# A transformer block on one core: channels in the order quad, dimension, head, a scratch layout to match, and another order of work ahead of the first quad

## The reference, cut to what matters

```python
x: (2, 1024, 128); 16 heads of 8
xn = layernorm(x)
Q, K, V = split_heads(xn @ wq.T), split_heads(xn @ wk.T), split_heads(xn @ wv.T)
Q, K = rope(Q), rope(K)                      # pairs (2f, 2f+1) of a head's 8 channels
attn = softmax(where(causal, Q K^T / sqrt(8), -inf))
out = x + (attn V) merged @ wo.T + (xn @ CB.T) * (SCB / 127) + bias
```

## Time and profile before

| | us |
|---|---|
| median of 3 runs | 284.9 (284.44 to 287.26) |
| profiled execution, its time | 284.91 |
| its span in the profile | 283.2 |
| mean granted TensorE clock | 0.994 of 2.4 GHz |

### The profile page before, as it was taken

How to read it: one execution, slowest core, us unless ns; L and a number is a source line. 1 busy time by engine, 2 the same in 40 slices (tenths; PEclk the granted TensorE clock), 3 DMA queues, 4 the chain that set the end, 5 groups by cost and what they waited for, 6 DMA issues and landing times.

```text
span 283.2 us, 11098 instructions
## 1 busy us (share of the span) xinstructions
PE 252.2 (89%) x4752; PEld 133.6 (47%) x4752; DVE 211.7 (75%) x601; ACT 188.6 (67%) x366; POOL 110.5 (39%) x170
## 2 busy tenths in 40 slices
PE   0785869759999999999999999999999999999875
PEld 0342644124334545554454554455455446666574
DVE  5897367878999899899798998988997783111123
ACT  0336423419877698779798789778988886888201
POOL 7634990499006561437440232043024014301200
PEclk9999999989999999999999999999999999999999
DMA  7415757480003450340043052005300000000011
GB/s 209 171 37 147 197 117 135 100 222 5 1 2 101 123 106 3 84 92 5 2 114 61 3 124 55 3 2 121 55 5 3 2 3 7 21 22 23 21 38 40
DMA packets 21497, 18.29 MB, mean 65 GB/s; under 512 B 2996, under 2 KB 20788, under 8 KB 21448
## 3 DMA queue, kind: packets, MB, share of 16 engines
q1 hardware_dynamic: 20872, 17.00, 25.1%
q10 hardware_dynamic: 576, 0.59, 0.7%
HBM read 12.12 MB, written 5.24 MB: 61 GB/s over the span
## 4 chain that ended last, share of the span: by engine, by line
PE 69%; DVE 13%; POOL 6%; DMA 5%; SPq 3%; ACT 2%; issue 2%; ACTq 0%; DVEq 0%
PE psV L908 21%; PE psB L840 19%; PE psA L840 18%; PE psA L943 7%; DVE prod L738 7%; DMA k_scratch<-ot 2%; DVE xn L696 2%; POOL xnT L440 2%; POOL ot L433 2%; SPq L336 2%; PE psB L823 1%; DMA x_sb<-x 1%; SPq L350 1%; DMA ks<-k_scratch 1%; DVE on L759 1%
## 5 line engine op out<-in xcount | busy, mean ns | idle before, releaser
L738 DVE CUSTOM_DVE_ANT_0 prod<-psA,cmask 128x128 f32<-128x128 f32 (+7 forms) x256 | 178.9, 755 | 28.8 <-PE psA L840 27.6
L641 ACT ACTIVATE ring<-psB 128x512 f32<-128x512 f32 x288 | 155.5, 601 | 33.2 <-PE psB L840 30.8
L840 PE MATMUL psB<-qs,ks 128*32 128x512 bf16 (+3 forms) x1536 | 101.7, 329 | 0.5 <-ACT maxT L600 0.4
L840 PE MATMUL psA<-ks,qs 128*32 128x512 bf16 (+3 forms) x1536 | 92.3, 330 | 7.9 <-DVE mx L738 4.3
L908 PE MATMUL psV<-ring,va 128*32 128x512 f32 (+3 forms) x768 | 76.1, 486 | 0.0
L487 POOL TENSOR_SCALAR_AFFINE_SELECT ring<-ring 128x512 f32<-128x512 f32 x64 | 39.9, 636 | 76.6 <-ACT ring L641 76.4
L840 PEld LDWEIGHTS psB<-qs,ks 128*32 128x32 bf16 x1536 | 41.3, 97 | 47.1 <-ACT ring L641 20.7
L840 PEld LDWEIGHTS psA<-ks,qs 128*32 128x32 bf16 x1536 | 34.0, 97 | 44.6 <-DVE mx L738 23.8
L908 PEld LDWEIGHTS psV<-ring,va 128*32 128x32 f32 x768 | 22.2, 110 | 16.0 <-issue 8.0
L467 POOL CAST shiftsT<-maxT 16x128 bf16<-16x128 f32 x16 | 4.5, 281 | 56.4 <-ACT maxT L633 50.1
L738 DVE DVE_READ_ACCUMULATOR2_ANT mx<- 128x1 f32 x256 | 21.4, 83 | 0.0
(11 more groups left out here) (88 smaller groups left out, 169.1 us busy)
## 6 DMA issues: line engine op xcount, KB each, us to landing
qs<-q_scratch SPq DMA_DIRECT2D x48, 96.0 KB
ks<-k_scratch SPq DMA_DIRECT2D x48, 96.0 KB
q_scratch<-ot SPq DMA_DIRECT2D x20, 128.0 KB, 2.7
k_scratch<-ot SPq DMA_DIRECT2D x12, 128.0 KB, 2.7
x_sb<-x SPq DMA_DIRECT2D x4, 256.0 KB, 4.6
rope_sb<-rope SPq DMA_DIRECT2D x2, 512.0 KB, 6.1
y<-xn SPq DMA_DIRECT2D x8, 128.0 KB, 1.8
qs<-shiftsT SPq DMA_DIRECT2D x32, 4.0 KB, 1.7
```

The source lines that it names most:

```text
L641: act.activation(ring[:, s % P_RING, k * HALF:(k + 1) * HALF], bank_b(e % B_RING), ACT.Exp)\
L738: last = dve.tensor_tensor_reduce(masked_scores[:, u % 2, at:at + w], psA[:, (u % 2) * SEQ + at:(u % 2) * SEQ + at + w], cmask[:, SEQ - w: ...
L840: mm = pe.matmul(psum[strip:strip + STRIP, at:at + size], keys[:, strip:strip + STRIP], queries, start=True, stop=True)
```

## The change

- *Channels.* Within the 128 channels of Q and K the order becomes quad, dimension, head (`rows` in the host's weights, the rope table with it). The scratch tensors become [token block, quad, part, 32 channels, 512 tokens], so that for one dimension the 4 heads are consecutive and a stack's row is one piece of 4 KB in DRAM.
- *Stores.* Each part is written once: 6 transfers a round, [4 quads, 32, 512].
- *Loads.* A half stack is 4 transfers: one per query part with its 8 rows repeated to 24 by a broadcast source, and one for the keys, 24 rows repeated to 72.
- *Order.* The weights 4 to 6, `scb` and `bias` are issued by SP behind rope, not by ACT. PE projects round 0 before it turns group 1, and does the first task (now V of batch 0) before groups 2 and 3. DVE normalises groups 2 and 3 between the rotations. POOL makes `cmask` first, scales the FFN's weights between the third and fourth rstd, and has pads of slots 1 and 2 and `va` behind the third parts. The tasks' table and `TASK_AFTER` are rewritten.

```diff
-TASKS = [("late", 4), ("late", 5), ("v", 0), ("v", 1), ("ffn", 0), ("ffn", 1), ("late", 6), ("max", 0), ("late", 7),
+TASKS = [("v", 0), ("ffn", 0), ("late", 4), ("late", 5), ("v", 1), ("ffn", 1), ("late", 6), ("max", 0), ("late", 7),
...
-        scratch = (nc.dram_tensor("q_scratch", [HEADS, PARTS + 2, DH, BATCH * SEQ], BF16),
-                   nc.dram_tensor("k_scratch", [HEADS, PARTS, DH, BATCH * SEQ], BF16))
+        scratch = [nc.dram_tensor(f"{name}_scratch", [BATCH * SEQ // HALF, HEADS // QUAD, PARTS, DH * QUAD, HALF], BF16)
+                   for name in ("q", "k")]
...
-            return 16 * (2 * PARTS * (i // SLOTS + 1) + i // SLOTS)
+            return 16 * (STACK_DMAS * (i // SLOTS + 1) + i // SLOTS)
...
-        ROUND_DMAS = 2 * PARTS + 2
+        ROUND_DMAS = 2 * PARTS
+        STACK_DMAS = PARTS + 1
...
-                for m in (n, PARTS + n) if c % 2 == 0 and n < 2 else (n,):
-                    sp.dma_start(scratch[c % 2][:, m, :, tok:tok + HALF], part(c, n)).then_inc(scratch_out[c // 2], 16)
+                sp.dma_start(scratch[c % 2][c // 2, :, n, :, :], part(c, n)).then_inc(scratch_out[c // 2], 16)
...
+                queries = scratch[0][block, rows, :, :, :].rearrange("p (d h) t -> p d (h t)", h=QUAD)
                 for g in range(PARTS):
-                    for source, first, stack in ((scratch[0], g, qs), (scratch[1], 0, ks)):
...
+                    sp.dma_start(qs[g * GROUP:(g + 1) * GROUP, slot, hf, :, :].rearrange("r h t -> r (h t)"),
+                                 queries[g, :, :].unsqueeze(0).to_broadcast([PARTS, DH, QUAD * HALF])).then_inc(ready, 16)
+                keys = scratch[1][block, rows, :, :, :].rearrange("p (d h) t -> (p d) (h t)", h=QUAD)
+                sp.dma_start(ks[0:STACK, slot, hf, :, :].rearrange("r h t -> r (h t)"),
+                             keys.unsqueeze(0).to_broadcast([PARTS, GROUP, QUAD * HALF])).then_inc(ready, 16)
...
             normalise(0)
+            normalise(1)
             statistics(2)
-            normalise(1)
-            statistics(3)
-            normalise(2)
-            normalise(3)
...
+            rotate(0)
+            rotate(1)
+            leave(0)
+            leave(1)
+            normalise(2)
+            statistics(3)
+            rotate(2)
+            normalise(3)
+            rotate(3)
+            leave(2)
+            leave(3)
...
             turn_rows(0)
-            turn_rows(1)
             pe.wait_ge(wq_scaled, 1)
             project_round(0)
+            turn_rows(1)
             project_round(1)
...
+        d = ch // QUAD % DH
...
+    rows = np.arange(P).reshape(HEADS // QUAD, QUAD, DH).transpose(0, 2, 1).reshape(P)
+    swap = rows ^ 1
```

More of the change, by code:

```diff
@@ L264, in attention_ffn_kernel @@
         cb_scaled = sem("cb_scaled")
+        va_set = sem("va_set")
         ln_step = sem("ln_step")
@@ L329, in _ @@
                 sp.dma_start(rope_sb[:, :, cols], rope[:, :, cols]).then_inc(rope_in[half], 16)
+            sp.dma_start(w_sb[:, 4:7, :], weights[:, 4:7, :]).then_inc(w_late_in, 16)
+            sp.dma_start(scb_sb[:, :], scb.partition_broadcast(P)).then_inc(vec_in, 16)
+            sp.dma_start(bias_sb[:, :], bias.partition_broadcast(P)).then_inc(vec_in, 16)
             def store_part(c, n):
-                tok = c // 2 * HALF
                 sp.wait_ge((part1, part2, part3)[n], c + 1)
-                for m in (n, PARTS + n) if c % 2 == 0 and n < 2 else (n,):
-                    sp.dma_start(scratch[c % 2][:, m, :, tok:tok + HALF], part(c, n)).then_inc(scratch_out[c // 2], 16)
+                sp.dma_start(scratch[c % 2][c // 2, :, n, :, :], part(c, n)).then_inc(scratch_out[c // 2], 16)
             def store_parts(r):
@@ L344, in load_stack @@
             def load_stack(i, hf):
-                slot, heads, tok = i % SLOTS, slice((i % 4) * QUAD, (i % 4 + 1) * QUAD), (i // 4) * SEQ + hf * HALF
+                slot, rows, block = i % SLOTS, i % 4, (i // 4) * 2 + hf
                 ready = stack_in[slot][hf]
+                queries = scratch[0][block, rows, :, :, :].rearrange("p (d h) t -> p d (h t)", h=QUAD)
                 for g in range(PARTS):
-                    for source, first, stack in ((scratch[0], g, qs), (scratch[1], 0, ks)):
-                        sp.dma_start(stack[g * GROUP:(g + 1) * GROUP, slot, hf, :, :],
-                                     source[heads, first:first + PARTS, :, tok:tok + HALF]
-                                     .rearrange("h p d t -> (p d) h t")).then_inc(ready, 16)
+                    sp.dma_start(qs[g * GROUP:(g + 1) * GROUP, slot, hf, :, :].rearrange("r h t -> r (h t)"),
[3 more added lines that the diff above has]
+                             keys.unsqueeze(0).to_broadcast([PARTS, GROUP, QUAD * HALF])).then_inc(ready, 16)
                 if i >= SLOTS:
@@ L413, in _ @@
             pads(qs, 0, 0.0, pads0_ready)
-            pads(qs, 1, 0.0, pads_ready)
+            pool.memset(cmask[:, :], 0.0).then_inc(cmask_ready, 1)
+            pool.wait_ge(cmask_ready, 1)
+            pool.affine_select(out=cmask[:, SEQ - P:SEQ], in_=cmask[:, SEQ - P:SEQ],
+                               compare_op=ALU.is_ge, fill=LOWEST, base=0, pattern=[[-1, P]],
+                               channel_multiplier=1).then_inc(cmask_ready, 1)
             for g in range(4):
@@ L420, in _ @@
                 pool.tensor_tensor(rstd[:, bt], var_eps[:, bt], exponent[:, bt], ALU.pow).then_inc(rstd_ready, 1)
[L421 to L426, removed]
+                if g == 2:
+                    pool.wait_ge(vec_in, 32)
+                    pool.wait_ge(w_late_in, 16)
+                    pool.tensor_scalar(scb_sb[:, :], scb_sb[:, :], 1.0 / 127.0, None, ALU.mult).then_inc(cb_scaled, 1)
+                    pool.wait_ge(cb_scaled, 1)
+                    pool.tensor_tensor(w_sb[:, 6, :], w_sb[:, 6, :], scb_sb[:, :], ALU.mult).then_inc(cb_scaled, 1)
             def third_part(c):
@@ L452, in _ @@
             third_part(3)
-            pads(qs, 2, 0.0, pads_ready)
-            pads(ks, 2, TWO_MINUS_ONES, pads_ready)
+            for slot in (1, 2):
+                pads(qs, slot, 0.0, pads_ready)
+                pads(ks, slot, TWO_MINUS_ONES, pads_ready)
+            pool.memset(va[:, :, :, :], 0.0).then_inc(va_set, 1)
+            pool.wait_ge(va_set, 1)
+            pool.memset(va[:, :, :, DH:DH + 1], 1.0).then_inc(va_set, 1)
             for half in range(2):
@@ L613, in _ @@
             turned_rows(1)
[L614 to L621, removed]
+            for n in range(2):
+                parts_of(0, n)
+                parts_of(1, n)
+            save_task(0)
+            turned_rows(2)
+            parts_of(2, 0)
+            turned_rows(3)
+            parts_of(3, 0)
+            parts_of(2, 1)
+            parts_of(3, 1)
+            for n in range(1, len(TASKS) - 1):
                 save_task(n)
@@ L715, in leave, with rotate @@
                                   ALU.subtract).then_inc(rest1, 1)
-            for c in range(LATE):
+            def rotate(c):
                 r, w = divmod(c, 2)
@@ L811, in task @@
                 if m == 0:
-                    pe.wait_ge(xnT_ready, 4 if n else 3)
+                    pe.wait_ge(xnT_ready, 4 if n else 2)
                     if n >= 2:
@@ L924, in beside @@
                             values(i, s)
-            for n in range(FIRST_TASKS):
-                for m in range(2):
-                    task(n, m)
+            task(0, 0)
+            task(0, 1)
+            turn_rows(2)
+            turn_rows(3)
+            task(1, 0)
+            task(1, 1)
+            task(2, 0)
+            task(2, 1)
             pe.wait_ge(products, 8)
@@ L937, in _ @@
             pe.wait_ge(task_saved, len(TASKS))
-            pe.wait_ge(cb_scaled, 4)
+            pe.wait_ge(va_set, 2)
             def turn_tile(to, tile, moving):
@@ L1021, in rope_tables @@
     for ch in range(P):
-        f = (ch % DH) // 2
-        table[ch, 0] = cos[:, f]
-        table[ch, 1] = sin[:, f] if ch % 2 else -sin[:, f]
+        d = ch // QUAD % DH
+        table[ch, 0] = cos[:, d // 2]
+        table[ch, 1] = sin[:, d // 2] if d % 2 else -sin[:, d // 2]
     return table
@@ L1030 @@
     from concourse.bass_utils import run_bass_kernel_spmd
-    swap = np.arange(P) ^ 1
+    rows = np.arange(P).reshape(HEADS // QUAD, QUAD, DH).transpose(0, 2, 1).reshape(P)
+    swap = rows ^ 1
     wq, wk = np.asarray(L0_attn_wq), np.asarray(L0_attn_wk)
-    weights = np.stack([wq.T, wq[swap].T, wk.T, wk[swap].T, np.asarray(L0_attn_wv).T,
+    weights = np.stack([wq[rows].T, wq[swap].T, wk[rows].T, wk[swap].T, np.asarray(L0_attn_wv).T,
                         np.asarray(L0_attn_wo).T, np.asarray(L0_ffn_CB).T], axis=1)
```

22 lines of the change are left out of this document (4 added, 18 removed).

## The result

| | before | after |
|---|---|---|
| median of 4 runs, us | 285.82 (284.44 to 287.26) | 318.38 (316.37 to 319.06) |
| profiled execution, time and span | 284.91, 283.2 | 316.37, 314.6 |
| mean granted clock of TensorE | 0.994 | 0.935 of 2.4 GHz |
| small packets (under 512 B) | 2,996 | 1,620 |

The changed kernel takes 1.1117 times as long (95%: 1.105 to 1.1184), 11% slower, 32.6 us. 320 was forecast.

A forecast was written before the change was run, and what follows sets the result against it. PE was taken to bound the long middle, SP's queue and the DMA engines behind it the front. Span 283.2 + 33.5 + 1.5 = 318.2, plus 1.7 around it, gave 319.9, say 320 us; range 300 to 338, its own 308 to 334.

The forecast's parts named there:

- Engines per transfer: All DMA transfers: the largest number up to 16 dividing both sides' outermost counts; 3 engines per load, 4 per store.
- The price by bytes: DMA transfers: about 2 us + bytes / 436 GB/s each; by that alone the change could only help the loads.
- R: Data time of one half-stack load on 3 engines: 8.2 us, bad end 14.4; the chain holds six.
- S: Data time of one 128 KB store on 4 engines: 1.8 us, between 1.36 and 2.0; the chain holds 12.75.
- Front: Up to PE's first scores: POOL's wait loses 1.8 us, third parts end at 25.0, first scores come near 38.6.
- From the second half to the shifted bank: Quad 0's second half to its shifted scores: both 17 us late; two more half tasks, 0.5 each, hidden.
- Shift rows: Quad 0's half 1 rows: issued near 83, queued behind loads and stores, landed 102.9, 33.5 us late; PE idles some 16.
- Sum: Whole kernel: 33.5 us late plus 1.5 gives span 318.2; with 1.7 around it 319.9, say 320.
- the 1.5 for the restart: After PE's idle wait for the shift rows: 1.5 us added for the lower granted clock.
- 1: Rival: engines counted on the SBUF side, loads keep 12 and stores 16; 286 us, or 284 with faster loads; chance 0.11.
- 3: Rival: loads and stores both narrow, with 14.4 us per half-stack load; 360 to 380 us, chance 0.04.
- Rival 2: Only one kind of transfer narrow: loads alone 303 us, stores alone 8 us late, 294; chance 0.06 together.

The follow-up runs named there:

- both wide forms: The changed kernel with only its stores widened to 16 engines (302.5 us, 1,908 small packets), or only its loads widened to 8 (304.2 us, 2,196).
- order_only: The changed kernel's order of work with the channels, scratch and transfers of the kernel before: 290.2 us, ratio 1.0167 to the kernel before.
- third_first: The changed kernel with POOL's fourth rstd moved behind the first two third parts: 317.5 us, ratio 1.1136 to the kernel before.
- layout_only: The order of work of the kernel before with the changed channels, scratch and transfers on 3 and 4 engines: 316.3 us, ratio 1.1086.
- wide_tasks: wide_both with the `TASK_AFTER` of the kernel before: 289.7 us, ratio 1.0154 to the kernel before.
- wide_old_order: The order of work of the kernel before with the new layout's transfers widened to 8 and 16 engines: 286.4 us, ratio 1.0047.
- the two half wide kernels: The changed kernel with only stores on 16 engines (302.5 us, ratio 1.0608), and with only loads on 8 engines (304.2 us, ratio 1.0675).
- shift_first: The changed kernel with quad 0's half 1 shift rows issued ahead of quad 2's loads and round 2's stores: 313.3 us, ratio 1.0993.
- wide_both: The changed kernel with stores on 16 engines and loads on 8, everything else as in the change: 292.4 us, ratio 1.0263.

## Why the prediction was right, step by step

**Engines per transfer.** Right, and exactly: 1,620 small packets forecast and measured, and the counts of both wide forms follow from the same rule. The reason given, that each engine needs its share on both sides, is not tested. The Trainium skill (DMA: Bandwidth & Descriptors, "Why a DMA increments its semaphore by 16 and not by 1") states this rule and, in "Rules for kernel authors", what a leading broadcast does; the traces agree, with 3 engines at a share of 0.19. The price by bytes that the prediction set against it stands on the same page of the Trainium skill in "Anatomy of one DMA — SWDGE (gpsimd) path", as a fit for transfers issued by GpSimd: about 2.0 us + bytes / 436 GB/s. By it an estimate for the 576 KB of a half stack is 3.4 us. The trace does not agree: load (0, 1) took 10.4 us from its first issue to its landing.

**R and S.** Forecast R = 8.2 and S = 1.8. Measured by the rates, a half stack of 589,824 B at 80 GB/s is R = 7.4, a store of 131,072 B at 88 GB/s S = 1.5. The six stores that follow load (0, 0) were landed 8.0 after it, where 10.8 was taken. But load (0, 1), which found its engines empty, started slowly, which the forecast had not:

```profile
49.00:52.00 3.00, 0.00 (x0) 0.00 (x0) 0.00 (x0) 0.00 (x0) 1.76 (x2) 0.79 0.16 41
```

Load (0, 1) moved 41 GB/s in its first 3 us and 80 after. From its first issue to its landing it is 10.4 us (47.98 to 58.41); less the 1.6 for start and landing, R is 8.8, and for load (0, 0) 9.1 or so. So in the sum two loads were 0.6 and 0.9 too cheap, four 0.8 too dear, and 12.75 stores 0.3 each: 5.5 us too much on the chain. The choice of 24.1 GB/s per engine over the old loads' 13.7 was right, since it is 26.7. The reason given was the longer rows, 4 KB instead of 1 KB; the number of engines changed with them, from 12 to 3, and no run parts the two.

**Front.** Third parts forecast at 25.0, measured 25.2; last store of round 0 landed at 29.1 (28.8); first scores at 40.0 (38.6). The second half came at 58.45 (59.2). That POOL's wait costs 1.8 is right where the transfers are not narrow (order_only's first half is 33.45 against 31.59). In the changed kernel it was counted in full as well, though the stores' own queue would have set nearly the same time: third_first shows this. The number came out, one of its causes did not.

**From the second half to the shifted bank.** Here the forecast failed. It said 17 us late at both ends, and put two more half tasks at 0.5 each, "also hidden" by the late second half. They lie behind that second half, so nothing hides them. Measured: 24.4 us against 19.4. With before's order, layout_only needs 22.6, so the order of work is about 1.8 of the 5.0, where the forecast had 1 for two more half tasks. The other 3.2 are there although the order is before's; the forecast had no term for them. In layout_only, as after, PE came to this stretch from a long wait (8.3 us there, 10.6 after), and its granted clock was 0.50, the level of 1.2 GHz, for the first 6 us and again for the last 5:

```profile
59.00:65.00 6.00, 5.66 (x34) 2.82 (x34) 2.41 (x6) 1.09 (x2) 0.00 (x0) 0.50 0.19 79
...
77.00:82.00 5.00, 2.91 (x26) 0.46 (x22) 3.85 (x8) 0.27 (x1) 4.92 (x5) 0.50 0.22 84
```

With the same `TASK_AFTER`, wide_tasks, at 1.00 throughout, does it in 19.4, and wide_old_order, at the low level for part of it, in 21.4. That the lower clock makes the 3.2 us is the likely reading; no run changed the clock alone.

**Shift rows.** Forecast landed at 102.9, 33.5 late; measured 99.07, 29.7 late. PE waits at the step where it was expected to, but for 8.2 us and not for some 16: the shifted scores start 3.8 later than forecast (82.81 against 79) and the rows come 3.8 earlier. The way was partly another. The forecast had the rows issued near 83 and waiting in the engines' queue for 20 us. In fact they were ready at 86.94, and SP was held up in its own issues until 92.02. Both are the same backlog, seen from two places.

**Sum.** 33.5 + 1.5 were forecast, 29.7 + 1.7 measured in the span; behind the last wait the granted clock is 0.50 for the first 3 us (99 to 102), as the 1.5 for the restart has it. Of the 5.5 us too much for R and S, 0.3 went into a later last store of round 0 and about 1.3 into a pause between quad 1's and quad 2's loads, which the forecast lets follow each other without a gap: 26 and 33 GB/s in the two us from 73, where 80 is the rate. That leaves the 3.8 by which the shift rows came earlier than forecast, within 0.1. That 320 lies so near to 318.4 is partly luck: the profiled execution, whose terms these are, is the fastest of the four, 316.4, and against it the forecast is 3.5 too long. The forecast's own range of 308 to 334 is also wider than the terms that it names, which reach from 310 to 326.

**Rivals.** 1 and 3 are out by the count and by R. Rival 2 can be held against the two half wide kernels. For narrow loads alone it has 303, and 302.5 was measured, though without a term for the longer stretch (23.3 us there too). For narrow stores alone it has 294, and 304.2 was measured, 10 short: the second half comes 2.5 later than it says (53.17 against 50.7), the stretch is 3.9 longer, and the shift rows' wait, 2.0, is missing.

## What to carry to other kernels

Before a transfer's pattern is changed, write down the outermost count of both its sides. In all twelve kernels here the largest number up to 16 that divides both fits the number of engines that carry it, and the profile's count of packets under 512 B tells it afterwards, one for each engine and transfer. A broadcast or a short block index belongs inside, the rows outside: fewer and longer transfers on a quarter of the engines lost 26 us here. A DMA share that is low and flat near 3/16 or 4/16 while engines wait for a DMA was a narrow queue here, not a free one, and everything behind it in that queue (here the tiny shift rows) paid as well.

## What the runs showed of the hardware

- In the kernel after, one engine carried on average 26.7 GB/s from DRAM in rows of 4 KB (3 engines, 80 GB/s) and 22.0 GB/s to DRAM in rows of 1 KB (4 engines, 88 GB/s).
- A load on 3 engines that found them empty moved only about half its rate in its first 3 us (41 of 80 GB/s, seen in load (0, 1) after).
- An issue on SP's queue was held up where the engines behind it had a backlog. A store's issue has a median of 0.6 to 0.7 us in most kernels (0.9 in shift_first), but its longest is 4.8 after, 4.6 in shift_first and 6.4 in layout_only, against 1.5 before, 1.4 and 1.8 in the two half wide kernels, 1.0 in wide_both and 2.1 in wide_tasks. What it is that is full was not tested.
- The price of an issue depends on the pattern: 0.38 us for an old load, 0.68 to 0.75 for a new one, 0.65 for the wide form. Four new issues take 2.9 us where six old ones took 2.5, so that fewer transfers saved nothing on SP either.
